# Order of TensorE's work at an item's start: the last state sum, the convolution's second half and z's projection

## The reference

```
xi, z = split(chunk @ in_proj_w.T)                 # 256 channels each
xc = silu(causal depthwise conv(xi, 4 taps) + conv_b)
dt, B, C = split(xc @ x_proj_w.T)                  # 8, 16, 16
dt = softplus(dt @ dt_proj_w.T + dt_proj_b)
for each token t and each of the 16 states s:
    h[s] = exp(dt * A[s]) * h[s] + dt * xc * B[s]
    y    = sum over s of h[s] * C[s]
y = (y + xc * D) * silu(z)
out = y @ out_proj_w.T + skip * chunk
```

## Time and profile before

| | us |
|---|---|
| runs: median of 3 | 16086.48 |
| runs: lowest, highest | 16082.97, 16089.99 |
| profiled execution: its own time | 16090.54 |
| profiled execution: span from first to last instruction | 16088.7 |
| TensorE's mean granted clock in it | 0.947 of full |

### The profile page before, as it was taken

The page is one execution under the profiler, slowest core; times in us unless marked ns, Lnnn a source line. Parts: engine busy times, 40 slices in busy tenths (PEclk is TensorE's granted clock), DMA queues, the critical chain, the costliest instruction groups (busy, mean ns, idle before and its releaser), DMA issues. The chain is left out here.

```text
span 16088.7 us, 151421 instructions
## 1 busy us (share of the span) xinstructions
PE 14186.2 (88%) x30720; PEld 5741.6 (36%) x30720; DVE 14823.6 (92%) x13024; ACT 11509.9 (72%) x18891; POOL 14788.2 (92%) x6275
## 2 busy tenths in 40 slices
PE   6988989889898898888889888899888898888888
PEld 2333333333333333333333333333333333333333
DVE  6999999999999999999999999999999999999998
ACT  5777767777677767777677776777767777677776
POOL 5999989999899989999899998999989999899998
PEclk8999999999999999999999999999999999999999
DMA  3444444444444444444444444444444444444444
GB/s 131 156 163 163 159 153 162 162 164 153 157 157 160 163 155 158 159 160 169 150 156 162 157 169 149 158 163 161 163 148 161 164 160 166 150 153 164 156 154 139
DMA packets 739082, 2537.63 MB, mean 158 GB/s; under 512 B 77241, under 2 KB 78017, under 8 KB 721729
## 3 DMA queue, kind: packets, MB, share of 16 engines
q1 hardware_dynamic: 738112, 2527.45, 46.1%
HBM read 2376.15 MB, written 150.99 MB: 157 GB/s over the span
## 5 line engine op out<-in xcount | busy, mean ns | idle before, releaser
L1460 POOL TENSOR_TENSOR RING<-RING,CS 128x1024 f32<-128x1024 f32 x4096 | 9597.9, 2363 | 1036.2 <-DVE RING L1150 973.3
L1150 DVE TENSOR_TENSOR_SCAN RING<-DA,HS,RING 128x512 f32<-128x512 f32 x8192 | 9946.1, 1265 | 496.9 <-ACT DA L777 451.1
L388 PE MATMUL YP<-RING,EYE 128*128 128x512 f32 x16384 | 8172.0, 632 | 1400.6 <-POOL RING L1460 1307.3
L777 ACT ACTIVATE DA<-ITEM,AN 128x512 f32<-128x512 f32 x8192 | 5495.8, 684 | 3017.5 <-DVE RING L1150 3001.5
L388 PEld LDWEIGHTS YP<-RING,EYE 128*128 128x128 f32 x16384 | 3126.8, 198 | 5995.0 <-issue 3596.3
L1130 DVE TENSOR_TENSOR RING<-DTP,BS 128x1024 f32<-128x1024 f32 x3072 | 3687.7, 1205 | 129.0 <-ACT DTP L847 117.6
L1447 POOL TENSOR_TENSOR RING<-ITEM,BS 128x1024 f32<-128x1024 f32 x1024 | 2421.3, 2365 | 10.0 <-DMA BS<-bc_rows 0.3
L388 PE MATMUL FL<-XN,WC 128*128 128x512 f32 x4096 | 1913.9, 611 | 9.8 <-ACT XN L866 4.6
L388 PEld LDWEIGHTS FL<-XN,WC 128*128 128x128 f32 x4096 | 821.4, 201 | 1087.4 <-issue 1079.1
L791 ACT ACTIVATE ITEM<-FL,COL 128x512 f32<-128x512 f32 x512 | 348.9, 682 | 1056.8 <-PE FL L388 1056.6
L388 PE MATMUL FL<-LS,WP 128*128 128x512 f32 x2048 | 983.2, 603 | 6.1 <-POOL LS L1482 6.1
(11 more groups left out here) (125 smaller groups left out, 10879.3 us busy)
## 6 DMA issues: line engine op xcount, KB each, us to landing
BS<-bc_rows SPq DMA_DIRECT2D x2048, 512.0 KB, 4.9
CS<-bc_rows SPq DMA_DIRECT2D x2048, 512.0 KB, 3.6
XR<-in_x SPq DMA_DIRECT2D x128, 1024.0 KB, 7.6
x_slices<-XR SPq DMA_DIRECT2D x64, 1024.0 KB, 8.3
XR<-x_slices SPq DMA_DIRECT2D x64, 1024.0 KB, 7.6
out<-XR SPq DMA_DIRECT2D x64, 1024.0 KB, 8.1
XR<-in_wqkv SPq DMA_DIRECT2D x24, 1024.0 KB, 7.8
bc_rows<-ROWS SPq DMA_DIRECT2D x256, 64.0 KB, 4.5
```

Of the source, the lines that this page charges most:

```text
L388: return pe.matmul(*a, **k)
L777: act.activation(DA[:, h, :], DT[:, i % 2, h, :], ACT.Exp, scale=AN[:, h, s:s + 1]).then_inc(dA_ready, 1)
L1150: dve.tensor_tensor_scan(H[:, slot(n), h, :], DA[:, h, :], U[:, slot(n), h, :], HS[:, i % ITEMS, h, s:s + 1], ALU.mult, ALU.add).then_inc( ...
L1460: pool.tensor_tensor(G[:, slot(n)], H[:, slot(n)], CS[:, s % C_ROWS, :].unsqueeze(1).broadcast_to([P, NH, T]), ALU.mult).then_inc(g_ready, 1)
```

## The change

In TensorE's `window` two calls move; nothing else is touched.

```diff
-                        if s == d:
+                        if s == 1:
                             if j == 0 and coming is not None:
                                 pe.wait_ge(v_ready_att, coming * 2 + 1)
                             xi_second(tile, w, first, ln2)
-                        if s == 2 + d:
+                        if s == 3 and d:
                             z_both(tile, w + 1)
...
                     if s > 1:
                         state_sum(tile, n - 2, first=first and s == 2)
+                    if front and s == 2 and not d:
+                        z_both(tile, w + 1)
```

## The result

The changed kernel takes 16244.25 us (median of 4 runs, 16240.35 to 16249.43) against 16084.72 us for the kernel before on the same chip: a ratio of 1.0100 with a 95% interval of 1.0083 to 1.0118, 159.5 us slower. Its profiled execution took 16249.43 us with a span of 16247.6 us, 158.9 us longer than that of before.

The account below looks back on a forecast made before the run. No single engine bounds it; behind the later half ScalarE's chain sets the time and GpSimd passes lateness on. Terms 54 + 10 - 14 + 45 + 16 = +111 us give 16197 us, forecast range 16130 to 16260, overall 16090 to 16290.

Parts of the forecast that it names:

- (a): j = 0 windows, sum 15 ahead of the half: VectorE's whole 2.16 us gate wait for TensorE is gone.
- (b): j = 0 windows, half 2.2 us later: ScalarE's copy is late, new 1.6 us wait at step 3, step 4 scans 0.9 us later.
- 1.3 us of slack: Ordinary d = 0 windows: step 4's exponentials are ready at 5158.03 and wanted at 5159.34; only delay beyond this makes scans late.
- j = 0 term: Step 4 lateness passed on to GpSimd: 57 windows x 0.9 plus 7 x 0.4 = +54 us.
- rival 3: z becomes the bound too, TensorE's clock could add: 185 windows by 0.5 to 1 us, +200 to +300 us; chance 0.1.
- j = 1: Step 4 scans 0.2 us late in 50 windows, +10 us; 14 statistics windows gain 1.0 us each, -14 us.
- j = 2: Steps 5 and 6 late, 43 x 1.05 = +45 us; behind statistics z waits for the gate, 14 x 1.15 = +16 us.
- hidden with 0.8 us to spare: z behind sum 0 costs nothing in j = 0 windows, covered by ScalarE's table load and first silu.
- j = 3: Windows with d = 1 keep their order, so no cost was forecast: 0 us.
- rival 2: Lateness is taken up by GpSimd's 109 us without idle time and VectorE's later waits: within 32 us of before; chance 0.15.
- precedent: j = 3 windows already have the new order: gate waits 0.00 us, step 5 scans wait 2.02 us for exponentials; an upper bound.
- rule on table loads: A switch costs about 2.66 us: no slack on ScalarE, whole 2.2 us comes through, some +370 us; the rows were followed instead.

Follow-up runs that it names:

- the opposite order: Kernel before with the convolution's second half ahead of sum 14 in windows with d = 0, z as before: 16078.9 us against 16079.0, ratio 1.0001.
- its first part alone: Kernel before with the half behind sum 15 in windows with j = 1 alone, z as before: 16058.1 us against 16081.8, ratio 0.9986.
- the best kernel: Kernel before with both halves early, in j = 3 windows of ordinary tiles, and the half behind sum 15 in j = 1 windows: 15956.5 us, ratio 0.9924.

## Why the prediction was right

**The sign and its mechanism** held step by step. (a) The gate's wait goes: 2.16 to 0.00 us. (b) The half is late, ScalarE's chain behind it uses up 1.3 us of slack and step 4 comes 0.9 us later: 0.96 us measured, with the stall of 1.6 us forecast at step 3 (1.80). The j = 0 term was +54 us and is +55. The sign of the change turns when the chain is shortened, and a delay of 1.04 us on ScalarE alone is free while 2.08 us is not; so slack and chain are shown, not only argued.

**The size** was low by 48 us: +111 forecast, +159 measured. What was missing is mostly TensorE's clock, which no term of the sum had and which rival 3 mentioned only in passing; that j = 1 came out cheaper hid part of it. The terms:

- j = 2, +61 forecast and +102 measured. In the 14 windows behind statistics I had 1.15 us. The two at full clock measured 1.18, so the chain was as described (sum 0 waits for the gate, z behind it). The 12 at a lower clock measured 2.7 to 2.9, 36 us in all where I had 16. In the ordinary windows z was priced at nothing, "hidden with 0.8 us to spare", and that holds; but the centring waits 28 us longer than in the kernel before, in the windows in which TensorE's clock is down.
- j = 3, 0 forecast and +17 measured. I left these windows out because their order does not change. Their step 5 waits 2.0 us in 36 windows of the changed kernel (8 before) and 1.2 us in 6 (29 before): the second half is later by 0.8 us there, behind sums at a lower clock. The clock granted in steps 0 and 1 is 0.89 and 0.85 in the 36 windows and 1.00 in the 6.
- j = 1, -4 forecast and -28 measured. The 14 statistics windows gain 3.0 us each and not 1.0: besides the gate their later waits shrink too, and I had read the gain at step 4 alone. The other 50 lose 14 us, where I had 10.

That j = 0 agrees to 1 us is in part luck: the time from the scans of step 0 to those of the next window, another way to cut the same kind out, is 61 us longer and not 55. A slip in rival 2 changes nothing: its "109 us without idle time" of GpSimd should be some 124 us by the earlier trace rows.

**The precedent** of the j = 3 window, which had the new order already and waited at ScalarE in place of the gate, pointed the right way and was the cheapest evidence of all.

**The rule on table loads** (the Trainium skill, ScalarE: Activation LUTs, What ACT_TABLE_LOAD costs) would have given +370 us with 2.66 us for a switch. The rows' 1.28 us and the threshold between 1.04 and 2.08 us of added work fit a slack of 1.3 us, which a switch of 2.66 us does not leave.

**What I had not seen** is that the gate and the copy are two entries to the same chain. It did not hurt the forecast, as the change moves the copy late and the gate early; it sank my expectation for the opposite order.

## What to carry to other kernels

A long wait in the list of an engine at 92% is worth nothing until you have followed what stands in for it: here 473 us of waiting at the gate, the longest wait of VectorE for another engine, hid a second chain with only 1.3 us of slack, and moving work out of the gate's way put it in the way of that chain. When two consumers want one engine at the same moment, look for an idle stretch of that engine ahead of both rather than swap their order. Price a moved step window kind by window kind; the changed order cost 55 us of VectorE's time in one, its first part alone gained 24 us in another, and the best kernel uses it only there.

## What the runs showed of the hardware

TensorE's granted clock differed at the same place of the program. Stretches of the timeline, with the columns span, busy time and count for PE, PEld, DVE, ACT and POOL, granted clock, DMA share, GB/s: the changed kernel's sum 0 and z behind statistics, and its sums 13 and 14 at the start of a j = 3 window; below, the same two places of the kernel before (at the first, sum 0 is followed by sum 1 there and not by z, as many instructions of the same shape).

```profile
5572.50:5577.70 5.20, 5.17 (x8) 2.20 (x9) 5.20 (x5) 2.12 (x2) 5.20 (x4) 0.67 0.68 185
...
3115.20:3120.40 5.20, 5.18 (x8) 2.15 (x9) 5.20 (x5) 2.20 (x4) 5.02 (x3) 0.67 0.55 205
```
```profile
5521.10:5524.70 3.60, 3.55 (x8) 1.44 (x8) 3.60 (x4) 3.57 (x4) 3.60 (x3) 1.00 0.59 171
...
3082.90:3087.00 4.10, 3.77 (x8) 1.53 (x9) 4.10 (x5) 1.51 (x3) 4.10 (x2) 1.00 0.75 238
```

Part of each slower stretch ran at 1.2 GHz, all of the faster ones at 2.4 GHz: eight matmul instructions take 5.2 us in place of 3.6 (in the last row 4.1, with a pause of 0.33 us). At the first place TensorE had stood idle 2.31 us ahead of it in the changed kernel and 0.81 us in the kernel before. At the second it had stood idle 2.64 us in both, and only one of them lost the clock; so the idle time just ahead does not settle it. Nor does it at the first place: in the window of the 1.18 us wait TensorE had stood idle 2.32 us and kept the full clock. At the centring shown above it fell with no pause over 0.84 us in the 30 us ahead. What settles it stays open here. Over the span the mean hardly moves (0.947 and 0.945), but the slower stretches lie on the path: 20 us more at z behind statistics, 28 us at the centring and 19 us at step 5 of j = 3 stand in the changed kernel's profiled execution at the lower clock.
